# Turning attention probabilities in 64-row halves side by side, with a step's waits on one semaphore instruction

## What is computed

```
q = _heads(seq_inputs @ Wq + bq)
k = _heads(seq_inputs @ Wk + bk)
v = _heads(seq_inputs @ Wv + bv)
scores = jnp.einsum('bhqd,bhkd->bhqk', q, k) / np.sqrt(HEAD_SIZE)
bias = jnp.where(graph_mask, 0.0, NEG)[:, None]
probs = jax.nn.softmax(scores + bias, axis=-1)
ctx = jnp.einsum('bhqk,bhkd->bhqd', probs, v)
ctx = ctx.transpose(0, 2, 1, 3).reshape(seq_inputs.shape[0], seq_inputs.shape[1], H)
return ctx @ Wf + bf
```

## Time and profile before

| | |
|---|---|
| median of three runs | 1814.38 us |
| the profiled execution, its own time | 1814.55 us |
| its span, first to last instruction | 1812.7 us |
| TensorE matmul busy | 96% of the span |
| VectorE, ScalarE, GpSimd busy | 74%, 61%, 57% |
| share of TensorE in the chain that ended last | 84% |
| granted TensorE clock, mean | 0.99 |
| bytes moved over the span | 25 GB/s |

### The profile page before, as it was taken

How to read it: one execution, slowest core, us unless ns; L and a number is a source line. 1 busy time by engine, 2 the same in 40 slices (tenths; PEclk the granted TensorE clock), 3 DMA queues, 4 the chain that set the end, 5 groups by cost and what they waited for, 6 DMA issues and landing times.

```text
span 1812.7 us, 36503 instructions
## 1 busy us (share of the span) xinstructions
PE 1743.6 (96%) x10992; PEld 1075.9 (59%) x10992; DVE 1340.8 (74%) x3130; ACT 1103.0 (61%) x2231; POOL 1033.6 (57%) x1287
## 2 busy tenths in 40 slices
PE   5899999999999999999999999999999999999985
PEld 4565656657465675646657565575656656566561
DVE  4668687786878768677786877868777686876847
ACT  3666565675666656566665656656566665666643
POOL 4356565673656656465564646646565565655635
PEclk9899999999999999999999999999999999999998
DMA  4000101001010010100001010010100101000000
GB/s 154 18 18 12 48 6 35 17 14 43 6 44 14 13 39 6 52 6 19 33 10 48 6 35 23 9 43 6 52 6 13 39 7 51 6 17 18 10 9 18
DMA packets 38112, 46.43 MB, mean 26 GB/s; under 512 B 2624, under 2 KB 38080, under 8 KB 38080
## 3 DMA queue, kind: packets, MB, share of 16 engines
q1 hardware_dynamic: 38080, 46.03, 7.9%
HBM read 33.44 MB, written 12.58 MB: 25 GB/s over the span
## 4 chain that ended last, share of the span: by engine, by line
PE 84%; DVE 7%; ACT 4%; issue 3%; POOL 1%; DVEq 0%; DMA 0%; POOLq 0%; ACTq 0%
PE work L1093 16%; PE score L1093 16%; PE acc L1176 9%; PE work L1161 9%; PE acc L1244 8%; PE score L1150 7%; PE acc L1238 6%; DVE arena L861 4%; ACT arena L572 3%; PE work L1238 3%; PE score L1219 2%; PE score L1108 2%; PE acc L1197 2%; PE score L1205 1%; PE work L1257 1%
## 5 line engine op out<-in xcount | busy, mean ns | idle before, releaser
L861 DVE SCALAR_TENSOR_TENSOR arena<-score,uqT,adjT 128x512 f32<-128x512 f32 x576 | 389.1, 743 | 35.7 <-PE score L1219 25.4
L414 POOL TENSOR_SCALAR arena<-arena,rinv 128x512 f32<-128x512 f32 x384 | 281.9, 750 | 183.8 <-DVE rinv L823 183.8
L572 ACT ACTIVATE arena<-sm,nmax 128x512 f32<-128x512 f32 x384 | 273.3, 713 | 132.2 <-DVE nmax L817 132.1
L817 DVE CUSTOM_DVE_ANT_0 sm<-score,mask 128x512 f32<-128x512 f32 x384 | 247.9, 686 | 67.9 <-PE score L1150 65.6
L448 POOL TENSOR_TENSOR arena<-arena,adjT 128x512 f32<-128x512 f32 x192 | 223.9, 1166 | 126.0 <-ACT arena L612 121.7
L1161 PEld LDWEIGHTS work<-ident_f,arena 128*128 128x128 f32 x1536 | 166.8, 141 | 127.5 <-DVE arena L827 80.3
L1161 PE MATMUL work<-ident_f,arena 128*128 128x128 f32 x1536 | 215.4, 280 | 6.2 <-POOL arena L414 3.1
L421 POOL TENSOR_TENSOR rstd<-var,mhalf 128x1 f32<-128x1 f32 x128 | 68.7, 549 | 233.0 <-DVE var L781 233.0
L1244 PE MATMUL acc<-arena,u_den 128*3 128x512 f32 x1536 | 200.8, 592 | 0.0
L1176 PE MATMUL acc<-arena,v_tok 128*64 128x512 f32 x768 | 198.9, 613 | 0.0
L609 ACT ACTIVATE arena<-score,nqT 128x512 f32<-128x512 f32 x192 | 129.9, 677 | 103.2 <-PE score L1219 75.7
(11 more groups left out here) (168 smaller groups left out, 3951.4 us busy)
## 6 DMA issues: line engine op xcount, KB each, us to landing
x_in<-in_x SPq DMA_DIRECT2D x16, 768.0 KB, 4.7
xb<-in_x SPq DMA_DIRECT2D x16, 768.0 KB, 4.6
out_x<-xres SPq DMA_DIRECT2D x64, 192.0 KB, 1.9
adj_u<-in_adj SPq DMA_DIRECT2D x16, 256.0 KB, 2.8
arena<-in_wk SPq DMA_DIRECT2D x1, 576.0 KB, 5.1
arena<-in_wq SPq DMA_DIRECT2D x1, 576.0 KB, 6.2
arena<-in_wv SPq DMA_DIRECT2D x1, 576.0 KB, 7.5
arena<-in_wf SPq DMA_DIRECT2D x1, 576.0 KB, 8.5
```

The lines of the kernel that those rows point to most:

```text
L414: nc.gpsimd.tensor_scalar(pr, pr, rinv[:, p, t, i:i + 1], 1.0, ALU.mult, ALU.mult).then_inc(probs_ready, 1)
L572: nc.scalar.activation(probs[p % 2 * 2 + i][:, t], sm[:, n % NSM], ACT.Exp, scale=-1.0, bias=nmax[:, p, t, i:i + 1], accum_out=rsum[:, p, ...
L817: mark_drained(nc.vector.tensor_tensor_reduce(sm[:, n % NSM], bank_of(g, "s", p, t, i)[:], mask[:, t], 1.0, 3.0e38, ALU.add, ALU.min, nmax ...
L861: nc.vector.scalar_tensor_tensor(out=edge_at(n, j), in0=score[j][:], scalar=uqT[:, c, q:q + 1], in1=adjT[:, c], op0=ALU.max, op1=ALU.mult) ...
```

## The change

A turn now takes 64 rows of queries: the weights are 64 rows by 128 columns, the moving operand is the 64 by 64 corner of `ident_f`, the output 128 by 64. The halves alternate: half 0 (rows 0 to 63) goes to bank `work0`, half 1 (rows 64 to 127) to `work1`, so that two turns in a row use different halves of the array and different banks. There are 16 turns in a step in place of 8. Each bank holds both heads, and both are marked full only at the last turns. The copies write pieces of 64 queries through the view `pT_half`. All waits of a step (both banks, and with c = 0 the last of the pair's probabilities) stand ahead of a `settle` before the first turn.

```
             def pT_copy(b, p, c):
                 filled(act, b, "turn", p, c, 1)
-                mark_drained(nc.scalar.activation(pT[c % 2][:, 1], bank_of(b, "turn", p, c, 1)[:], ACT.Copy),
-                             b, "turn", p, c, 1)
+                mark_drained(nc.scalar.activation(
+                    pT_half[c % 2][:, :, 1], bank_of(b, "turn", p, c, 1).rearrange("p (a n) -> p a n", n=DH0),
+                    ACT.Copy), b, "turn", p, c, 1)
...
             def turn_probs(b, p, c):
+
+                for half in range(2):
+                    bank_free(pe, b, "turn", p, c, half)
+                if c == 0:
+                    pe.wait_ge(probs_ready, b * NS + tile_no(p, TT - 1, 1) + 1)
+                settle(pe)
                 for i in range(2):
-                    bank_free(pe, b, "turn", p, c, i)
                     for t in range(TT):
-                        if c == 0:
-                            pe.wait_ge(probs_ready, b * NS + tile_no(p, t, i) + 1)
-                        ins = nc.tensor.transpose(bank_of(b, "turn", p, c, i)[:, t * P:(t + 1) * P],
-                                                  probs[p % 2 * 2 + i][:, t, c * P:(c + 1) * P], ident_f[:])
-                    mark_full(ins, b, "turn", p, c, i)
+                        for half in range(2):
+                            rows = slice(half * DH0, (half + 1) * DH0)
+                            at = (i * TT + t) * DH0
+                            ins = nc.tensor.transpose(bank_of(b, "turn", p, c, half)[:, at:at + DH0],
+                                                      probs[p % 2 * 2 + i][rows, t, c * P:(c + 1) * P],
+                                                      ident_f[rows, rows])
+                            if i == 1 and t == TT - 1:
+                                mark_full(ins, b, "turn", p, c, half)
```

More of the change, by code:

```diff
@@ L196, in build @@
         pT = [view(4 * k, 2, N) for k in range(2)]
+        pT_half = [view(4 * k, 2 * TT, 2, DH0) for k in range(2)]
         probs = [view(26 + 8 * i, TT, N) for i in range(4)]
@@ L566, in exps @@
                     if t == 0 and p == 2:
-                        filled(act, g, "turn", 0, TT - 1, i)
+                        if i == 0:
+                            filled(act, g, "turn", 0, TT - 1, 0)
+                            filled(act, g, "turn", 0, TT - 1, 1)
                     if p == 0 and t == 2 and i == 1 and not (isinstance(g, int) and g == 0):
@@ L826, in pT_copy @@
                 filled(dve, b, "turn", p, c, 0)
-                mark_drained(nc.vector.tensor_copy(pT[c % 2][:, 0], bank_of(b, "turn", p, c, 0)[:]),
-                             b, "turn", p, c, 0)
+                mark_drained(nc.vector.tensor_copy(
+                    pT_half[c % 2][:, :, 0], bank_of(b, "turn", p, c, 0).rearrange("p (a n) -> p a n", n=DH0)),
+                    b, "turn", p, c, 0)
             def ctx_low(b, p):
```

## The result

| | before | changed |
|---|---|---|
| median of four runs each | 1815.43 us | 1799.4 us |
| their range | 1814.37 to 1816.65 | 1798.65 to 1799.62 |
| span of the profiled execution | 1812.7 us | 1797.7 us |

The ratio is 0.9911, with a 95% interval of 0.9894 to 0.9928: faster by 0.9%, 16 us where 23 were forecast. The two spans differ by 15.0 us, or 0.94 us for each of the 16 turns of the loop.

A forecast was written before the change was run, and what follows sets the result against it. TensorE was taken as the bound, with VectorE just under it in pairs 0 and 1. Savings of 0.6 us there and 0.85 in pair 2, 1.45 over 16 graphs, made 23 us: 1791 us, range 1765 to 1826.

The forecast's parts named there:

- The step of turns: Turns ahead of scores: sixteen half turns would take 0.53 us a step in place of 0.87, saving 0.34.
- Pair 2: Last pair of the loop's turn, where TensorE alone sets the pace: four steps save 0.85 us, all passed on.
- So of 8 x 0.34 = 2.7 us, about 0.6 arrives: Pairs 0 and 1: copies hold most steps, so only 0.6 us of the eight steps' full saving reaches K(0).
- So this is hidden, just: T(0,0): scores start 0.22 us later, but VectorE's earlier maxima and copy, until 825.15, cover the delay.
- 0.08 of release: Held steps such as T(0,1): 0.08 us from the end of ScalarE's copy to the turns, then 0.53 of turns.
- 0.23 + 0.33 = 0.56 us earlier than before: Pairs 0 and 1: VectorE's idle before the maxima of S(2,0) and S(2,2) goes, moving later work 0.56 us earlier.
- A: Experiments' theory: VectorE and ScalarE are full in pairs 0 and 1, so shorter turns gain little there.
- B: Experiments' rival theory: the missing gain is paid on TensorE, at the new semaphore instruction with its longer release.
- All of it arrives: Rival: copies do not hold pairs 0 and 1, 65 us saved, 1749 us; over 36 us faster had chance 0.06.
- nothing changes: Rival: later T(0,0), copy holds and queuing take back pair 2's gain; 1811 to 1818 us, chance 0.10.
- single file: Rival: the sixteen turns come one after another, 0.061 us each, 0.98 a step; 40 us slower, 1855, chance 0.13.
- the load sets the pace: Rival: weight loads keep a pair of turns at 0.108 us, a step at 0.87; 1838 us, chance 0.05.

The follow-up runs named there:

- e4: Changed kernel with all eight turns of half 0 first, then the eight of half 1, in place of alternating halves; 1826.56 us.
- e11: e7 with VectorE's copy of T(2,2) moved ahead of its correction of the next graph's key 1; 1785.85 us.
- e3: Changed kernel with the score product S(1,1) issued ahead of the turns T(0,0); 1794.33 us.
- e6: Changed kernel with three elementwise steps of the second layer's tail computed on only 8 of 384 columns, the rest left out; 1785.93 us.
- e7: e3 with the tail's steps for query block 2 moved on VectorE and ScalarE from within pair 1 to just before pair 2; 1789.29 us.
- e12: Changed kernel with three semaphore instructions in a row ahead of each step's turns in place of one; 1822.14 us.
- e9: e7 with ScalarE's copies of T(0,1) and T(1,0) each placed one exponential earlier; 1795.17 us.
- e2: Kernel before, with its full 128-row turns, but all waits of a step gathered at one semaphore instruction; 1845.45 us.

## Why the prediction was right, and where its size was off

The time lies in the range, and the mechanism is the one forecast: shorter steps, passed on in pair 2 and mostly turned into idle time in pairs 0 and 1. The gain is 16 us where 23 were forecast, and most of the difference lies in pairs 0 and 1.

**The step of turns.** 0.87 us became 0.50 ahead of scores (0.53 forecast). Starts in twos show where instructions are queued; after a release they come one by one 0.03 us apart, as taken from the earlier trace rows. The rate is the same either way. That turns alternating between the halves overlap is shown by e4.

**The copies.** 0.57 to 0.60 us on ScalarE and 0.67 to 0.69 on VectorE, as before: writing in pieces costs nothing.

**Pair 2.** 0.69 us by the medians; 0.73 in this turn of the loop, where the terms are:

| term | forecast | measured |
|---|---|---|
| T(2,0) | 0.16 | 0.07 |
| T(2,1) | 0.25 | 0.23 |
| T(2,2) | 0.34 | 0.35 |
| T(2,3) | 0.10 | 0.12 |
| C(2,2) to K(2) | 0 | -0.04 |

Most of what is missing stands in T(2,0). The forecast took its step of before at 0.87 us; between products of the keys, which use the full array as those turns did, it had been 0.79 (849.01 to 849.80 in the trace of before). Now it is 0.65 (841.80 to 842.45), and the entry from the keys went from 0.23 to 0.32 (841.48 to 841.80): 0.14 - 0.09 is left of the saving, 0.05 by these rounded starts. T(2,3) was held by VectorE's copy for 0.19 us, as forecast, and e11 shows that it was this copy.

**Pairs 0 and 1: the term that was mis-sized** is "So of 8 x 0.34 = 2.7 us, about 0.6 arrives". 0.26 did. The mechanism under it, most of the saving turning into idle ahead of T, is in the trace. Three terms that it is made of were off.

- *"So this is hidden, just"*, of the 0.22 us by which T(0,0) ends later, was wrong. S(1,1) began at 817.13 + 7.03 = 824.16 (824.13 forecast), but VectorE's maxima came at 825.37 where its copy had ended at 825.14: 0.23 us of idle. The forecast set the start of the scores against the end of the copy. The scores take 0.97 us to the end of their last product (817.13 to 817.67 + 0.43), and the maxima start 0.24 us behind that end: 824.13 + 0.97 + 0.24 = 825.34, later than 825.15. e3 shows its worth: 0.25 us a turn of the loop. 0.26 + 0.25 = 0.51 is most of the 0.6.
- *"0.08 of release"* is 0.15: ScalarE's copy ends at 818.36 + 0.57 = 818.93 and T(0,1) starts at 819.08; GpSimd's last probability ends at 816.49 and T(0,0) starts at 816.63. What these 0.07 us more in each held step cost was not measured by itself.
- *"0.23 + 0.33 = 0.56 us earlier than before"* came to less than half: the maxima of S(2,0) stand at 833.85 (833.86 before), those of S(2,2) at 838.16 (838.34 before), and ScalarE's copy of T(1,2) at 843.27 (843.52 before). The idle ahead of both maxima is gone, as forecast, but what follows T(0,1) and T(0,2) had come 0.12 and 0.45 us later than before, by the first two terms for a part, and VectorE's tail step in between took 0.81 us where it took 0.57 at the same place before (at 835.09). I didn't test why it is longer.

The 0.25 us of that last copy is all that reaches K(0), and the rows show by which way. The first row is C(1,3) in the kernel before; the others, in the changed kernel, are ScalarE's copy of T(1,2), VectorE's copy of T(1,3) and C(1,3):

```profile
845.79 0.65 PE L1176 MATMUL acc<-arena,v_tok 128*64 128x512 f32 x2
...
836.24 0.57 ACT L582 ACTIVATE arena<-work 128x512 f32<-128x512 f32 x1
837.70 0.68 DVE L832 COPY arena<-work 128x512 f32<-128x512 f32 x1
838.51 0.65 PE L1190 MATMUL acc<-arena,v_tok 128*64 128x512 f32 x2
```

C(1,3) starts 0.13 us after VectorE's copy of T(1,3) ends, before (844.98 + 0.68 = 845.66, then 845.79) and after (838.38, then 838.51), so in both kernels K(0) waits for that copy and not for TensorE's own work. In the changed kernel it starts at 837.70, when the turns of T(1,3) are through (836.96 + 0.71 = 837.67); these wait 0.30 us for ScalarE's copy of T(1,2), and so does, by way of ScalarE's next instruction, the work that stands ahead of the copy on VectorE. Of the prediction's signs, then, idle ahead of T stands at T(0,1), T(0,2), T(1,1) and T(1,3) but not at T(1,2), and VectorE's waits for scores are not nearly gone: the two named ones went, and one of 0.23 us came.

**The theories.** Neither A nor B alone holds. Work taken off VectorE and ScalarE brings gains (e6, e7), and twice those of the kernel before, but less than A alone says and not in pair 0; delay added on TensorE costs (e12), though A makes most of it free. As I read the rows, after the change the three engines hold each other in pairs 0 and 1 in a ring: copy, turns, scores, maxima, exponentials, and the next copy behind them. Relief on one side gives a part; a change of order as in e9 takes from one what it gives the other.

**The rivals.** "All of it arrives" is off by the windows; "nothing changes" (1811 to 1818) by the time, 1799.4; "single file" and "the load sets the pace" by the step's 0.50 us, and a queued pair every 0.06. The Trainium skill's rule of a load of 107 ns for 128 columns ("TensorE: Matmul & The Clock Gate", section "LDWEIGHTS (loading the stationary operand)") does not hold as their pace: in e4 loads of 128 columns follow each other every 0.06 us within one half.

**Why pair 0 keeps its 12.4 us** in e6, with less work on VectorE and ScalarE, can be read from the changed kernel's trace, though no run tests it. ScalarE works without a gap from 819.07, when the maxima of S(1,1) are out, through four exponentials and the copy of T(0,1), to 822.49; T(0,2) starts at 822.63, and from there the trace shows no idle time of TensorE until T(1,0) at 829.12. The tail's first step in this stretch comes later, on VectorE at 822.73, so taking it away frees nothing on this way: T(0,0) to T(0,2) is 6.00 us in the changed kernel and in e6.

**What stays open.** The halves without the semaphore instruction were not tried, nor the halves in one bank, nor full turns in two banks by turns. How the last 0.09 us of the forecast 0.6 divide between the release and the longer tail step isn't known.

## What to carry to other kernels

Small fp32 turns of 64 rows pay most where they truly alternate between the halves of the array (and here between two banks); eight of one half and then eight of the other lost 27 us, more than the change had won. Before gathering a step's waits into one, look at what the second half of the step waited for: everything ahead of it now comes after that wait, and without shorter turns this cost 30 us. When a delay is said to be hidden, compare the end of the late work and the release behind it, not its start, with the end of the cover; and where three engines hold each other up, an engine's idle time in front of a step is neither free to fill nor a sum to be won.

## What the runs showed of the hardware

- A semaphore increment on TensorE holds the queue for 0.151 us until the next one, and 0.08 until a weight load (e12). From the end of the releasing work to the first turn behind it, it is 0.14 to 0.15 us (T(0,0) and T(0,1) of the changed kernel).
- Turns of 64 rows by 128 weight columns and 64 moving ones come every 0.06 us in one half (e4), and two per 0.06 us when halves and banks alternate (T(2,0) of the changed kernel).
- Going from the full array to one cut in halves costs about 0.09 us: T(2,0) begins 0.32 us after the last product of the keys, where the full turns began 0.23 after it (848.78 to 849.01 before). It isn't the semaphore instruction: e2 has it with full turns, and its pair 2 takes 12.08 us for 12.09.
- A copy that writes its 512 columns in eight pieces of 64 takes no longer than one that writes them in a row: 0.57 to 0.60 us on ScalarE and 0.67 to 0.69 on VectorE, before and after.
